# Half of the relu rounds of a recommendation tower move from ScalarE to VectorE, added to the round before

## The chip, the cores and the metric

The kernel runs on one core of a Trainium2 chip. Its time is the device time of one execution in microseconds; smaller is better. The time before is the median of three runs. One more execution was taken by the hardware profiler, and all rows below come from that one.

## The reference

2,048 samples, 16 fields each. Every field looks up a row of 256 floats in its own table, so a sample is a matrix `x` of 16 x 256. Three layers work on it:

```
xk = x
for i in range(3):
    z = einsum('bfe,bge->bfge', x, xk).reshape(B, 256, E)      # pairwise products of fields
    z = swapaxes(z, 1, 2)
    z = einsum('bcl,oc->bol', z, Ws[i]) + bs[i][None, :, None]  # here E = 256 is contracted with Ws[i]
    z = sum(relu(z), axis=-1)                                   # 16 numbers a sample
    outs.append(z)
    xk = broadcast(z[:, :, None], (B, 16, 256))
h = concatenate(outs + [dense_ctx]); two relu layers (512, 256) and one output
```

Layer 0 needs the products of fields with each other. Layers 1 and 2 (in the kernel k = 0 and k = 1) multiply `x` by a number per sample and field, so they need only the projection of `x` by the weights, an outer product with the previous `z`, the bias, relu, and a sum over all 16 x 16 pairs.

## The kernel before

The batch is worked in 128 steps of 16 samples; 8 steps make a group of 128 samples, 16 groups in all. All arithmetic is f32. The program is a hand-written software pipeline: each engine runs its own loop over "slots" 0 to 159, and in slot s it does its share for step s and, at fixed offsets, its share of the later stages of earlier groups. Engines meet only through semaphores; within an engine the order of the code is the order of execution. Because the offsets repeat every 8 slots, a slot's extra work depends on its number modulo 8.

For each step k:

- GpSimd gathers embedding rows by indirect DMA into `emb` (line 257), and does a small share of the products (lines 267 and 217).
- TensorE transposes them into the PSUM tile `turn_ps` (`turn`, line 483). It does this two slots ahead, as the first thing in its slot, and first waits until VectorE has done the products of the current slot, which read the same half of `turn_ps`.
- ScalarE copies `turn_ps` to `emb_t` (lines 398, 399) and makes the squares (line 406).
- VectorE makes the products (`products`, in `multiply`, line 217): 3,360 numbers per partition, one factor from `turn_ps` and one from `emb_t`.
- TensorE contracts them with the weights (`sum_pairs`, line 503, 32 matmuls), and ScalarE reduces the result with relu (`relu_pairs`, lines 416 and 419).

Layers 1 and 2 of a group are each cut into four rounds q = 0 to 3. In every slot from 14 on TensorE does one round (`outer_round`, lines 531 and 535): bias and outer product go into `outer_ps`, a PSUM tile of four banks of which only one copy exists, so the next round waits for `outer_relu`, the count of rounds already read. Round (k, g, q) is in slot 8g + 14 + q for k = 0 and 8g + 26 + q for k = 1, hence q = 1 and q = 3 always fall into odd slots. In the next slot ScalarE takes the result out with relu into `relu_k[:, k, q]` (`relu_round`, line 426; 4 x 256 numbers per partition). After the fourth round TensorE sums over rounds and over the four partitions that share a sample with a selector matrix `fold_sb` (`fold`, line 555) into `wide_ps`, and VectorE sums over fields (`reduce_fields`, line 369) into `z_cat`. GpSimd spreads `z_cat` into `z_wide` for the next layer (line 291).

`wide_ps` exists once. Its users follow each other in a fixed order, each waiting for the reader of the one before (`wait_wide`). By slot modulo 8:

| slot mod 8 | TensorE, beside turn, sums, one round | VectorE, behind `products` |
|---|---|---|
| 0 | `project` (line 546) | `reduce_fields` (k = 1) |
| 1 | `z_t` (line 517) ahead of the sums | `finish0` (lines 352, 355) |
| 2 | `fold` (k = 0) | `turn_proj` (line 363) |
| 3 | `z0` (line 514) ahead of the sums | |
| 4 | `hidden1` (line 563) | `reduce_fields` (k = 0) |
| 5 | `hidden2` (line 572) | |
| 6 | `fold` (k = 1) | |
| 7 | `y` (line 521) ahead of the sums | |

The order of an engine's slot is that of its loop. TensorE: `turn(slot + 2)`, side work, `sum_pairs(slot)`, `outer_round`, wide work. VectorE: `products(slot)`, then what the table's last column names. ScalarE reads the results of `hidden1` and `hidden2` one slot later (`relu_hidden`). ScalarE: `relu_round` of the slot before, `take_turned(slot + 2)`, `relu_hidden`, `squares(slot + 2)`, `relu_pairs(slot)`, side work. `prods` has three buffers. Products end with step 127; slots 128 to 159 only finish the last groups.

Of the kernel before, what the change touches and what calls it, by code (L numbers as in the profile page):

```python
# [11 lines left out]
ALU = mybir.AluOpType  # L12
# [7 lines left out]
F = 16  # L20
# [18 lines left out]
G4 = F // 4  # L39
# [20 lines left out]
ROUND_NO = {(k, g, q): n for n, (_, k, g, q) in enumerate(ROUND_ORDER)}  # L60
ROUND_AT = {s: (k, g, q) for s, k, g, q in ROUND_ORDER}
# [9 lines left out]
def group_at(slot, offset):  # L71

    g, rest = divmod(slot - offset, PER)
    return g if rest == 0 and 0 <= g < GROUPS else None


def at_least(eng, sem, value):

    if value > 0:
        eng.wait_ge(sem, value)  # L80


def build(nc, tables, ids_t, id_limits, ident, w_cols, biases, bias_rows, bias_parts, w_proj, own_field, row_mask,
          sample_mask, fold_sel, dense_t, w_top1, b_cols1, w_top2, b_cols2, w_top3, y_out):
    ctx = ExitStack()
    with ctx:
        def sb(name, shape, dt=FP32):
            return ctx.enter_context(nc.sbuf_tensor(name, shape, dt))

        def ps(name, shape):  # L90
            return ctx.enter_context(nc.psum_tensor(name, shape, FP32))

        def sem(name):
            return ctx.enter_context(nc.semaphore(name))
# [13 lines left out]
        relu_k = sb("relu_k", [P, 2, G4, J, F * F])  # L108
# [33 lines left out]
        outer_ps = ps("outer_ps", [P, J, 512])  # L142
# [30 lines left out]
        outer_done = sem("outer_done")  # L173
        outer_relu = sem("outer_relu")
        fold_done = [sem(f"fold_done{k}") for k in range(2)]
# [34 lines left out]
        def multiply(eng, k, b0, b1, own, done):  # L210

            x = emb_blocks(k)[:, b0:b1, :]
            step = [list(d) for d in x.ap]
            shifted = bass.AP(x.tensor, x.offset + 1, [step[0], step[1], [1, SHIFTS - 1], [1, F]])
            every = own.rearrange("p n (u f) -> p n u f", u=1).broadcast_to([P, b1 - b0, SHIFTS - 1, F])
            out = prod_blocks(k)[:, b0:b1, F:SHIFTS * F].rearrange("p n (s f) -> p n s f", f=F)
            eng.tensor_tensor(out, every, shifted, ALU.mult).then_inc(done, 1)  # L217
# [93 lines left out]
        def _(dve):  # L311
# [21 lines left out]
                                           in1=bias_part[:, 0, :], op0=ALU.mult, op1=ALU.add).then_inc(setup, 1)  # L333
            dve.wait_ge(setup, 9)
            nc.vector.scalar_tensor_tensor(out=rest_mid[:], in0=bias_lo[:], scalar=parts_sb[:, 2:3],
                                           in1=bias_part[:, 1, :], op0=ALU.mult, op1=ALU.add).then_inc(setup, 1)
# [4 lines left out]
            def products(k):  # L341

                if k < STEPS:
                    dve.wait_ge(emb_t_ready, 2 * (k + 1))
                    at_least(dve, sums_done, k - PRODS_RING + 1)
                    own = turn_ps[:, k % 2, :].rearrange("p (n f) -> p n f", f=F)[:, 0:VECTOR_BLOCKS, :]
                    multiply(nc.vector, k, 0, VECTOR_BLOCKS, own, prods_dve)

            def finish0(g):

                dve.wait_ge(relu0_ready, 3 * PER * (g + 1))
                nc.vector.tensor_reduce(own_sum[:], own0[:, g % 2, :, :], AX.X, ALU.add).then_inc(own_sum_ready, 1)
                dve.wait_ge(own_sum_ready, g + 1)
                at_least(dve, diag_ready, g - 1)
                nc.vector.scalar_tensor_tensor(out=z0_rows[:, g % 2, :], in0=pair_sum[:, g % 2, :], scalar=2.0,
                                               in1=own_sum[:], op0=ALU.mult, op1=ALU.add).then_inc(z0_ready, 1)

            def turn_proj(g):

                dve.wait_ge(proj_done, g + 1)  # L360
                if g >= PT_RING:
                    dve.wait_ge(outer_done, ROUND_NO[1, g - PT_RING, G4 - 1] + 1)
                nc.vector.transpose(proj_b[:, g % PT_RING, :].rearrange("p (f m) -> p f m", f=F),
                                    wide_ps[:].rearrange("p (s f) -> p f s", f=F)).then_inc(proj_ready, 1)

            def reduce_fields(k, g):

                dve.wait_ge(fold_done[k], g + 1)
                nc.vector.tensor_reduce(z_cat[:, g % CAT_RING, (k + 1) * F:(k + 2) * F],  # L369
                                        wide_ps[:, 0:F * F].rearrange("p (f o) -> p o f", o=F),  # L370
                                        AX.X, ALU.add).then_inc(z_ready[k], 1)

            for slot in range(LAST_SLOT + 1):
                products(slot)
                if (g := group_at(slot, Z0_FIN)) is not None:
                    finish0(g)
                if (g := group_at(slot, TURN_P)) is not None:
                    turn_proj(g)
                for k in range(2):
                    if (g := group_at(slot, REDUCE[k])) is not None:  # L380
                        reduce_fields(k, g)

        @block.scalar
        def _(act):
# [16 lines left out]
            def squares(k):  # L401

                if k < STEPS:
                    act.wait_ge(emb_t_ready, 2 * (k + 1))
                    at_least(act, sums_done, k - PRODS_RING + 1)
                    nc.scalar.square(prod_blocks(k)[:, :, 0:F], emb_blocks(k)[:, :, 0:F]).then_inc(squares_ready, 1)  # L406
# [15 lines left out]
            def relu_round(k, g, q):  # L422

                act.wait_ge(outer_done, ROUND_NO[k, g, q] + 1)
                at_least(act, fold_done[k], g)
                nc.scalar.activation(relu_k[:, k, q, :, :], outer_ps[:, :, 0:F * F], ACT.Relu).then_inc(outer_relu, 1)  # L426
# [32 lines left out]
            for slot in range(LAST_SLOT + 1):  # L459
                if slot == HIDDEN1:  # L460
                    act.wait_ge(top_in, N_TOP * 16)
                if slot - 1 in ROUND_AT:
                    relu_round(*ROUND_AT[slot - 1])
                take_turned(slot + 2)
                if slot - 1 in WIDE_AT:
                    relu_hidden(*WIDE_AT[slot - 1])
                squares(slot + 2)
                relu_pairs(slot)
                if slot in SIDE_AT:
                    take_side(*SIDE_AT[slot])  # L470

        @block.tensor
        def _(pe):
# [76 lines left out]
            def fold(k, g):  # L550

                pe.wait_ge(outer_relu, ROUND_NO[k, g, G4 - 1] + 1)
                for q in range(G4):
                    for j in range(J):
                        last = nc.tensor.matmul(wide_ps[j * R:(j + 1) * R, 0:F * F], fold_sb[:], relu_k[:, k, q, j, :],  # L555
                                                start=q == 0, stop=q == G4 - 1)
                last.then_inc(fold_done[k], 1)

            def hidden1(g):
# [96 lines left out]
```

## Time and profile before

| | us |
|---|---|
| median of 3 runs | 630.85 (630.07 to 631.62) |
| profiled execution, its own time | 628.34 |
| its span, first to last instruction | 626.6 |
| TensorE (PE) busy | 575.6 |
| VectorE (DVE) busy | 499.5 |
| ScalarE (ACT) busy | 455.3 |
| GpSimd (POOL) busy | 463.7 |

The span is what the trace covers; the execution's own time is 1.7 us longer. Busy times are of single engines and overlap each other. PEld, in some rows, is the load of weights into TensorE, beside the matmuls. "L217" is line 217 of the kernel before.

### The profile page before, as it was taken

What the parts mean: (1) busy time and instruction counts of PE and PEld (TensorE: products, weight loads), DVE (VectorE), ACT (ScalarE), POOL (GpSimd) and SP (SyncE); (2) the same over time, 40 slices, a digit from 0 to 9 for tenths busy, and PEclk for the clock granted to TensorE, in tenths of its full rate; (3) what the DMA queues carried; (4) which work ended last, traced back from release to release, by engine and by line L of the source; (5) the groups of instructions that cost most, each with busy time, mean ns of one, the idle gap of its engine ahead of it and who ended that gap; (6) DMA issues with size and microseconds to landing.
All of it is one profiled execution on the core that took longest, in us unless ns stands there. A gap on an engine that the chain in (4) does not pass through costs nothing.

```text
span 626.6 us, 19391 instructions
## 1 busy us (share of the span) xinstructions
PE 575.6 (92%) x7936; PEld 328.8 (52%) x7936; DVE 499.5 (80%) x220; ACT 455.3 (73%) x1298; POOL 463.7 (74%) x565
## 2 busy tenths in 40 slices
PE   2878798999999999999999999999999999997776
PEld 1444454555646555564656555565556555554354
DVE  5999999999898988889898988889888888941000
ACT  2666777787878787877887787777878788765542
POOL 6999999999988788888888888788878787621000
PEclk9999999999999999999999999999999999999988
DMA  3322222222222212222212122212212222100000
GB/s 97 112 73 73 69 70 68 70 70 65 69 64 61 61 58 63 61 61 62 65 56 65 57 61 60 69 55 68 60 55 67 61 61 57 47 3 1 1 1 2
DMA packets 14794, 35.97 MB, mean 57 GB/s; under 512 B 5922, under 2 KB 6306, under 8 KB 14690
## 3 DMA queue, kind: packets, MB, share of 16 engines
q0 software_dynamic: 12288, 33.57, 18.8%
q1 hardware_dynamic: 2418, 1.16, 0.7%
q8 instruction: 64, 1.05, 0.7%
q14 instruction: 24, 0.19, 0.1%
HBM read 34.70 MB, written 0.01 MB: 55 GB/s over the span
## 4 chain that ended last, share of the span: by engine, by line
PE 82%; POOL 8%; issue 4%; ACT 3%; DMA 1%; DVE 1%; SPq 0%; POOLq 0%
PE sum_ps L503 35%; PE turn_ps L483 10%; PE wide_ps L555 10%; PE outer_ps L535 8%; PE wide_ps L572 6%; PE wide_ps L546 4%; POOL emb L257 4%; PE outer_ps L531 4%; PE wide_ps L563 3%; POOL prods L267 2%; POOL prods L217 2%; ACT relu_k L426 1%; PE sum_ps L521 1%; PE sum_ps L517 1%; DVE prods L217 1%
## 5 line engine op out<-in xcount | busy, mean ns | idle before, releaser
L217 DVE TENSOR_TENSOR prods<-turn_ps,emb_t 128x3360 f32<-128x3360 f32 x128 | 466.1, 3655 | 55.1 <-ACT emb_t L399 52.2
L257 POOL DMA_INDIRECT emb<-tables,rows_sb x256 | 252.2, 985 | 45.4 <-issue 34.5
L503 PE MATMUL sum_ps<-prods,w_sb 128*32 128x272 f32 x4096 | 265.0, 397 | 18.6 <-POOL prods L217 11.1
L503 PEld LDWEIGHTS sum_ps<-prods,w_sb 128*32 128x32 f32 x4096 | 136.4, 110 | 103.6 <-issue 39.6
L426 ACT ACTIVATE relu_k<-outer_ps 128x1024 f32<-128x1024 f32 x128 | 132.4, 1035 | 11.2 <-PE outer_ps L535 11.1
L416 ACT ACTIVATE relu<-sum_ps,bias_sb 128x120 f32<-128x120 f32 x256 | 90.6, 361 | 58.4 <-PE sum_ps L503 57.2
L267 POOL TENSOR_TENSOR prods<-emb_t 128x256 f32<-128x256 f32 x128 | 95.3, 745 | 46.3 <-ACT emb_t L399 45.1
L398 ACT COPY emb_t<-turn_ps 128x512 f32<-128x512 f32 x128 | 75.3, 589 | 71.3 <-PE turn_ps L483 71.3
L483 PE MATMUL turn_ps<-ident_sb,emb 128*128 128x128 f32 x512 | 84.6, 289 | 12.7 <-DMA emb<-tables,rows_sb 10.0
L483 PEld LDWEIGHTS turn_ps<-ident_sb,emb 128*128 128x128 f32 x512 | 55.1, 142 | 60.5 <-issue 57.6
L406 ACT ACTIVATE prods<-emb_t 128x512 f32<-128x512 f32 x128 | 81.5, 637 | 3.3
L217 POOL TENSOR_TENSOR prods<-emb_t 128x224 f32<-128x224 f32 x128 | 77.5, 605 | 2.3
L535 PE MATMUL outer_ps<-proj_b,z_wide 32*128 32x256 f32 x1024 | 78.0, 378 | 0.0
L555 PE MATMUL wide_ps<-relu_k,fold_sb 128*32 128x256 f32 x1024 | 61.9, 382 | 1.5 <-ACT h L453 1.4
L291 POOL TENSOR_TENSOR z_wide<-z_cat,sample_sb 128x512 f32<-128x512 f32 x32 | 33.7, 1052 | 29.0 <-PE outer_ps L535 21.1
L369 DVE TENSOR_REDUCE z_cat<-wide_ps 128x16 f32<-128x256 f32 x32 | 13.4, 419 | 50.3 <-PE wide_ps L555 50.3
L416 ACT ACTIVATION_READ_ACCUMULATOR relu<-sum_ps,bias_sb 128x1 f32 x256 | 51.5, 201 | 0.0
L399 ACT COPY emb_t<-turn_ps 128x256 f32<-128x256 f32 x128 | 49.5, 386 | 0.0
L531 PE MATMUL outer_ps<-bias_wide,ones_sb 32*128 32x256 bf16 x512 | 37.0, 279 | 10.7 <-ACT relu_k L426 10.5
L531 PEld LDWEIGHTS outer_ps<-bias_wide,ones_sb 32*128 32x128 bf16 x512 | 12.9, 91 | 64.0 <-issue 52.7
L555 PEld LDWEIGHTS wide_ps<-relu_k,fold_sb 128*32 128x32 f32 x1024 | 30.3, 109 | 28.1 <-issue 9.3
L535 PEld LDWEIGHTS outer_ps<-proj_b,z_wide 32*128 32x128 f32 x1024 | 40.2, 186 | 0.0
(41 smaller groups left out, 284.3 us busy)
## 6 DMA issues: line engine op xcount, KB each, us to landing
emb<-tables,rows_sb POOLq DMA_INDIRECT x256
w_sb<-w_top SPq DMA_DIRECT2D x1, 512.0 KB, 4.3
ids_sb<-ids_t SPq DMA_DIRECT2D x1, 128.0 KB, 2.1
h<-dense_t SPq DMA_DIRECT2D x1, 128.0 KB, 2.9
w_sb<-w_top SPq DMA_DIRECT2D x1, 128.0 KB, 3.1
ident_sb<-ident SPq DMA_DIRECT2D x1, 64.0 KB, 2.1
w_sb<-w_cols SPq DMA_DIRECT2D x1, 64.0 KB, 1.9
wp_sb<-w_proj SPq DMA_DIRECT2D x1, 32.0 KB
```

Source lines behind the costliest of these rows:

```text
L217: eng.tensor_tensor(out, every, shifted, ALU.mult).then_inc(done, 1)
L257: nc.gpsimd.indirect_dma_start(out=emb[:, k % EMB_RING, t * E:(t + 1) * E], out_offset=None, in_=tables, in_offset=bass.IndirectOffsetOnAx ...
L267: nc.gpsimd.tensor_tensor(prod_blocks(k)[:, :, SHIFTS * F:], x[:, :, 0:SHIFTS], x[:, :, SHIFTS:F], ALU.mult).then_inc(prods_pool, 1)
L398: nc.scalar.copy(out[:, :, 0:F], src).then_inc(emb_t_ready, 1)
L406: nc.scalar.square(prod_blocks(k)[:, :, 0:F], emb_blocks(k)[:, :, 0:F]).then_inc(squares_ready, 1)
L416: nc.scalar.activation(relu0[:, t, :], sum_ps[:, t * PAIRS + F:(t + 1) * PAIRS], ACT.Relu, bias=bias_sb[:, 0:1], accum_out=pair_sum[:, g % ...
L426: nc.scalar.activation(relu_k[:, k, q, :, :], outer_ps[:, :, 0:F * F], ACT.Relu).then_inc(outer_relu, 1)
L483: last = nc.tensor.transpose(turn_ps[:, k % 2, i * P:(i + 1) * P], emb[:, k % EMB_RING, i * P:(i + 1) * P], ident_sb[:])
L503: last = nc.tensor.matmul(sum_ps[s * 2 * F:(s + 1) * 2 * F, 0:SUM_COLS], w_sb[:, c, odd, :], x[:, c, 2 * s + odd, :, :], start=c == 0 and ...
L531: nc.tensor.matmul(outer_ps[:, j, 0:F * F], ones_sb[j * R:(j + 1) * R, :], bias_wide[j * R:(j + 1) * R, k, :], start=True, stop=False)
L535: last = nc.tensor.matmul(outer_ps[:, j, 0:F * F], z_wide[j * R:(j + 1) * R, k, q, :], y[j * R:(j + 1) * R, k, :, :], start=False, stop=True)
L555: last = nc.tensor.matmul(wide_ps[j * R:(j + 1) * R, 0:F * F], fold_sb[:], relu_k[:, k, q, j, :], start=q == 0, stop=q == G4 - 1)
```

## The change

VectorE reads the rounds q = 1 and q = 3 out of `outer_ps`. One `scalar_tensor_tensor` takes the maximum with 0 and adds the relu of the round ahead, which ScalarE wrote to `relu_k[:, k, q - 1]`; the sum goes to `relu_k[:, k, q]`. It stands in VectorE's loop behind the products of the slot after the round. ScalarE keeps q = 0 and q = 2. `fold` reads only `relu_k[:, k, 1]` and `relu_k[:, k, 3]`, so 16 matmul instructions instead of 32 show for it in the trace.

```
+def on_vector(k, g, q):
+
+    return q % 2 == 1
...
+            def relu_add(k, g, q):
+
+                dve.wait_ge(outer_done, ROUND_NO[k, g, q] + 1)
+                dve.wait_ge(outer_relu, ROUND_NO[k, g, q])
+                at_least(dve, fold_done[k], g)
+                nc.vector.scalar_tensor_tensor(out=relu_k[:, k, q, :, :], in0=outer_ps[:, :, 0:F * F], scalar=0.0,
+                                               in1=relu_k[:, k, q - 1, :, :], op0=ALU.max, op1=ALU.add).then_inc(outer_relu, 1)
+
...
             for slot in range(LAST_SLOT + 1):
                 products(slot)
+                if slot - 1 in ROUND_AT and on_vector(*ROUND_AT[slot - 1]):
+                    relu_add(*ROUND_AT[slot - 1])
                 if (g := group_at(slot, Z0_FIN)) is not None:
...
-                if slot - 1 in ROUND_AT:
+                if slot - 1 in ROUND_AT and not on_vector(*ROUND_AT[slot - 1]):
                     relu_round(*ROUND_AT[slot - 1])
...
                 pe.wait_ge(outer_relu, ROUND_NO[k, g, G4 - 1] + 1)
-                for q in range(G4):
+                for q in range(1, G4, 2):
                     for j in range(J):
                         last = nc.tensor.matmul(wide_ps[j * R:(j + 1) * R, 0:F * F], fold_sb[:], relu_k[:, k, q, j, :],
-                                                start=q == 0, stop=q == G4 - 1)
+                                                start=q == 1, stop=q == G4 - 1)
```

## Rows read from the trace of the kernel before

**Rows 1.** The page's first part: busy us, share of the span, instructions.

```profile
PE 575.6 (92%) x7936; PEld 328.8 (52%) x7936; DVE 499.5 (80%) x220; ACT 455.3 (73%) x1298; POOL 463.7 (74%) x565
```

**Rows 2.** Waits, 175 to 547 us, TensorE's and VectorE's: us, times, longest.

```profile
PE sum_ps L503 <- ACT y_sb L439: 0.2, 1, 0.2
...
DVE prods L217 <- ACT emb_t L399: 44.2, 65, 1.4
```

**Rows 3.** Windows: length; busy PE, PEld, DVE, ACT, POOL; granted clock, DMA share, GB/s.

```profile
76.16:107.56 31.40, 27.79 (x402) 15.60 (x398) 30.53 (x14) 23.53 (x72) 28.58 (x35) 1.00 0.24 71
107.56:140.07 32.51, 32.27 (x482) 17.29 (x478) 31.14 (x14) 26.65 (x75) 29.70 (x37) 1.00 0.24 67
140.07:175.16 35.09, 34.88 (x496) 19.83 (x492) 31.02 (x14) 27.62 (x81) 31.82 (x39) 1.00 0.24 69
175.16:210.66 35.50, 35.28 (x504) 20.07 (x499) 31.09 (x14) 28.06 (x82) 28.93 (x35) 1.00 0.21 61
...
606.00:616.00 10.00, 9.14 (x76) 6.77 (x72) 0.34 (x1) 3.82 (x8) 0.00 (x0) 0.66 0.01 2
```

**Rows 4.** The chain, 300 to 345 us: start, duration, what.

```profile
302.01 0.59 PE turn_ps L483 x4
...
307.21 0.44 PE turn_ps L483 x4
...
310.27 1.86 PE wide_ps L555 x32
312.13 0.59 PE turn_ps L483 x4
...
315.74 0.59 PE turn_ps L483 x4
...
329.76 0.59 PE turn_ps L483 x4
...
333.10 0.58 PE turn_ps L483 x4
...
337.52 0.59 PE turn_ps L483 x4
```

**Rows 5.** Lines by form: shapes, count, busy us, mean ns, idle before.

```profile
L217 DVE TENSOR_TENSOR prods<-turn_ps,emb_t 128x3360 f32<-128x3360 f32 x128 | 466.1, 3655 | 55.1 <-ACT emb_t L399 52.2
...
L426 ACT ACTIVATE relu_k<-outer_ps 128x1024 f32<-128x1024 f32 x128 | 132.4, 1035 | 11.2 <-PE outer_ps L535 11.1
...
L369 DVE TENSOR_REDUCE z_cat<-wide_ps 128x16 f32<-128x256 f32 x32 | 13.4, 419 | 50.3 <-PE wide_ps L555 50.3
...
L332 DVE SCALAR_TENSOR_TENSOR bias_part<-bias_mid,parts_sb,bias_part 128x32 f32<-128x32 bf16 x1 | 0.3, 252 | 0.0
```

**Rows 6.** One line's instructions: duration in ns, least, median and greatest.

```profile
L355 DVE SCALAR_TENSOR_TENSOR z_rows<-pair_sum,own_sum x16: 174/176/555, 46.9 to 564.3; 128x16 f32<-128x16 f32 x16
```

**Rows 7.** Timeline of VectorE, early and at the last products: start, duration.

```profile
46.50 0.41 DVE L352 TENSOR_REDUCE own_sum<-own 128x16 f32<-128x256 f32 x1
...
47.03 3.65 DVE L217 TENSOR_TENSOR prods<-turn_ps,emb_t 128x3360 f32<-128x3360 f32 x1
50.60 0.71 DVE L363 STREAM_TRANSPOSE proj_b<-wide_ps 128x512 f32<-128x512 f32 x1
51.23 10.75 DVE L217 TENSOR_TENSOR prods<-turn_ps,emb_t 128x3360 f32<-128x3360 f32 x3
...
548.52 7.44 DVE L217 TENSOR_TENSOR prods<-turn_ps,emb_t 128x3360 f32<-128x3360 f32 x2 [0.33 <-ACT emb_t L399]
```

**Rows 8.** The chain, from the last sums to the end: start, duration, what.

```profile
560.78 2.01 PE sum_ps L503 x29
...
569.58 0.14 issue
...
570.45 1.86 PE wide_ps L555 x32
...
613.66 1.93 PE wide_ps L555 x32
```

## The prediction

> **What bounds the kernel now.** I read the page's busy row first [rows 1]: TensorE 92%, VectorE 80%, ScalarE 73%. Shares alone do not say who waits, so I took the table of waits over 175 to 547 us, where the kernel repeats itself [rows 2]. There TensorE waits 0.2 us in 372, VectorE 44.2 us, always for ScalarE's copy of the turned embeddings, which itself can only follow TensorE's turn. So TensorE is the bound in that stretch, and VectorE has slack. The windows, cut where VectorE starts `finish0` (once in 8 slots), say since when [rows 3]: 31.40 us, 32.51, 35.09, then 35.50 for every further 8 slots. In the first of these VectorE is busy 30.53 of 31.40, TensorE only 27.79; from the third on TensorE is full (34.88 of 35.09). The early part is thus already set by the product side (VectorE, GpSimd close behind), the long part by TensorE.
>
> The chain in the repeating part gives TensorE's slots [rows 4]. I call a slot by its number modulo 8; the distance between starts of its `turn` is its length. Slot 5 (its usual work, then `hidden2`) is 302.01 to 307.21, 5.20 us; slot 6 (`fold1`) 4.92; slot 7 (`y`, no wide work) 3.61; slot 3 329.76 to 333.10, 3.34; slot 4 4.42; all eight 302.01 to 337.52, 35.51.
>
> **Removed from TensorE.** A fold's 32 matmuls are 1.86 us of chain [rows 4] and become 16, 0.93. Two folds in 8 slots: TensorE's own period falls from 35.5 to 33.65. This is a true gain if TensorE stays the bound. Fewer reads of `relu_k` cost nothing elsewhere.
>
> **Removed from ScalarE.** 64 of 128 relus of 1.035 us [rows 5], 66 us. ScalarE was not the bound; its copies start when the turn ends, and I cost this at nothing: what hides it is TensorE's queue. In the new order VectorE's own queue hides it.
>
> **Added to VectorE.** 64 instructions over 128x1024 f32, one input in PSUM, one in SBUF. No such form is in the trace. From below: two VectorE operations that read PSUM give a slope of (3655 - 419) / (3360 - 256) = 1.0425 ns an element; 419 + 768 x 1.0425 = 1220 ns [rows 5]. From above: the same operation on 32 elements with a pointer scalar took 252 ns [rows 5], 219 beyond its elements, so 1.28 us. A duration under 1.035, ScalarE's own for this tile, has no row for it. I take 1.22, because this instruction has no pointer scalar. Back to back, VectorE starts the next instruction 0.08 us before the last one's end: products 47.03 to transpose 50.60 is 3.57 for 3.65, transpose to products 0.63 for 0.71 [rows 7]. So in the queue: products 3.57, new relu-and-sum 1.14, field reduction 0.33, transpose 0.63, `finish0` 0.53 (46.50 to 47.03 [rows 7]). Eight slots of VectorE, never waiting:
> 8 x 3.57 + 4 x 1.14 + 2 x 0.33 + 0.63 + 0.53 = 34.94 us.
> That is above TensorE's 33.65: VectorE becomes the bound, and the fold's saving is out of reach. By itself 34.94 would still be 0.56 less than 35.50.
>
> **The new wait.** The relu-and-sum of an odd slot's round stands on VectorE behind the products of the next slot and waits for TensorE's `outer_round`. Queued behind it are the next products, which TensorE's `turn` and `sum_pairs` need. So I followed one period, each engine in its order. TensorE in slot s starts its turn when the products of s are done, 0.13 to 0.14 us later (the 0.14 of "issue" ahead of TensorE in [rows 8]), or when its previous slot ends. I used the slot lengths above, with the fold shortened in slot 6 to 3.99; slots 0 to 2 together were 35.51 - 5.20 - 4.92 - 3.61 - 3.34 - 4.42 = 14.02 and are 13.09 now, against VectorE's 3 x 3.57 + 2 x 1.14 + 0.33 + 0.53 + 0.63 = 14.48.
> From slot 1 to slot 5 TensorE is thus ready before the products or just with them, and the round is done before VectorE gets to it. The closest is slot 3: its round ends 0.13 + 3.34 + 0.07 = 3.54 after its products' end, at 3.66 + 3.54 = 7.20 after their start; VectorE is free at 2 x 3.57 = 7.14. About 0.1 us of wait with a cold start of TensorE.
> Slot 5 is long (`hidden2`), and slot 6 has a fold. From the end of the products of slot 5, TensorE needs 0.13 + 5.20 + 3.99 + 3.61 + 0.07 = 13.00 us to the round of slot 7. VectorE gets there sooner: 3.57 + 1.14 + 3.57 + 3.57, less the 0.08 of overlap, = 11.77. It stalls some 1.2 us, once a period. What is late next: the reduction and the products of slot 1, then all of the queue up to the products of slot 5, for which TensorE waits. The loop closes:
> relu-and-sum 1.14, reduction 0.33, slot 1 3.57 + 0.53, slot 2 3.57 + 1.14 + 0.63, slot 3 3.57, slot 4 3.57 + 1.14 + 0.1 + 0.33, products of slot 5 3.66, then 13.00: 36.28 us.
> I take 36.3 against 35.5. The other waits of this edit are covered: `fold` needs the relu-and-sum 3.3 us after its slot's turn, and it and the transpose take 1.14 + 0.71; TensorE's `outer_round` needs it behind `sum_pairs` (2 us), and it takes 1.22. Both covers would fail only if it cost about 2 us. ScalarE's copies are ready over 1 us before VectorE asks.
>
> **The sum, against the profiled 628.34 (span 626.6).**
> Early, VectorE is full, so its work counts: the 8 slots to 76.16 get one of the new instructions, +1.1; the next 31.40 get two: busy 30.53 [rows 3] + 2.28 = 32.8, +1.4; the 32.51 get four, 34.9, +2.4. Together +4.9.
> From slot 34 to 127: 94 slots, 11.75 periods; the first 35.09 to 36.3, the other 10.75 by +0.8: 1.2 + 8.6 = +9.8.
> Behind the last products: VectorE ends them at 555.96 (548.52 + 7.44 [rows 7]), and TensorE ends the last sum at 562.79 (560.78 + 2.01 [rows 8]), 6.8 us behind, since it was the bound. With VectorE ahead by no more than one slot it is: slots 5 and 6 without their turns' 0.59 in slot 6, 0.13 + 5.20 + 3.40 + 0.42 + 2.0 = 11.15 after the products of slot 5; the last products end 8.28 after those. 2.9 behind, so -3.9.
> Tail: five folds on the chain, from 570.45 to 613.66 [rows 8], each -0.93, -4.65; of the relus there about five go to VectorE and pass on 1.22 instead of 1.035, +0.9. -3.7.
> Sum: 4.9 + 9.8 - 3.9 - 3.7 = +7.1. The profiled run lay 2.5 us under the median of 630.85; I add to the median: 638.0.
>
> **Rivals.**
> A. Queue order costs nothing: the stall behind slot 7 doesn't form, and the period is VectorE's bare 34.94. For it: TensorE has 34.94 - 33.65 = 1.3 us of slack in a period. Against: it is short in slots 5 to 7, where they come together. The two periods differ by 1.36 x 11.75 = 16.0: 622. This is the one on the other side; the break-even lies 7.1 / 11.75 = 0.60 under 36.3, at a period of 35.7: half of the stall would have to be absent.
> B. TensorE stays the bound, 33.65. It needs a relu-and-sum of (33.65 - 30.38) / 4 = 0.8 us in the queue, under every row: 2.65 x 11.75 = 31.1 less than mine, and 4.9 early, about 602.
> C. The new instruction runs at half the rate: 2.29 us, 1.07 more each. Three are in the loop: 39.5; 3.2 x 11.75 = 37.6, early 1 + 2 + 4 of them 7.5, five in the tail 5.3: 688. Against: the same operation with both inputs f32 in SBUF took 176 ns on 16 elements [rows 6]; at 1.04 ns an element the rest is 159, near the 152 of the reduction (419 - 267); at twice that, 143. That leans to full rate, by 17 ns only.
> The Trainium skill ("Vector Engine (DVE) Microarchitecture Reference", section "Points that are easy to get wrong") says that this instruction's layout halves its throughput with two SBUF sources that are not bf16. Here one source is in PSUM, so by its words the rule does not bite; if it holds for any second f32 source it gives C's time. The row of 176 ns, which has two such sources, does not agree with it clearly.
> D. Dearer hand-overs: no overlap at 1.28 us (+0.16 each, three in the loop) and 0.4 us of further restarts of TensorE: period 37.2, +0.9 x 11.75 = 10.6 and about 1.5 elsewhere: 650.
> That the change doesn't do what it says has no room: each operation stands in its engine's list.
>
> **Numbers.** Mine 0.60, own range 631 to 646; A 0.16; B 0.02; C 0.06; D 0.16. A and the low end of mine hold what ends faster or near zero. About 0.3% (2 us) is what a measurement here can tell from none. The relu-and-sum at 1.22 to 1.28 is +2.8 us on the sum, an overlap that fails +3.8. The tail may move too: TensorE's granted clock was 0.66 over 606 to 616 [rows 3], between its levels of 1.2 and 2.4 GHz; another pattern of waits there can be worth 2 or 3 us either way. Range 620 to 651, from A to D: outside lie C, B and edges. Faster 0.19 (A, B, a little of mine), same 0.09, slower 0.72.
>
> **What would show it.** VectorE busy about 577 us, over 90% of the span; the new line near 1.22 us; ScalarE near 389; the fold line with 512 matmuls and 31 us. In 175 to 547 us, TensorE should wait for VectorE's products several times a period, VectorE should be idle about 1.3 us a period, before the relu-and-sum, put down to `outer_round`; the 8-slot distance of `finish0` 36.3. The last sum should end about 3 us behind the last products. Wrong would make it: a period under 35.7, VectorE idle for ScalarE's copies as before, or another duration of the new line.

## The result and the profile after

The changed kernel took 654.79 us (median of 4, 653.66 to 656.76) against 630.8: 1.0383 of before, 95% interval 1.0354 to 1.0412, 24 us slower. The forecast was 638.0, up to 651. The direction was right and the loop that the forecast rests on is there, but the change cost over three times the 7.1 us that I had worked out. The same program, measured twice more, gave 1.0211 (1.0187 to 1.0235) and 1.0409 (1.0369 to 1.0449). About two thirds of what was missing is that difference, and the experiments below are mostly about it.

The busy row of the page and the forms that answer to [rows 1] and [rows 5]:

```profile
PE 553.2 (85%) x7424; PEld 308.2 (47%) x7424; DVE 566.2 (87%) x284; ACT 406.8 (62%) x1234; POOL 462.3 (71%) x565
```

```profile
L222 DVE TENSOR_TENSOR prods<-turn_ps,emb_t 128x3360 f32<-128x3360 f32 x128 | 461.9, 3644 | 3.0 <-ACT emb_t L414 3.0
L376 DVE SCALAR_TENSOR_TENSOR relu_k<-outer_ps,relu_k 128x1024 f32<-128x1024 f32 x64 | 78.3, 1224 | 57.2 <-PE outer_ps L550 57.1
...
L441 ACT ACTIVATE relu_k<-outer_ps 128x1024 f32<-128x1024 f32 x64 | 65.6, 1025 | 28.5 <-PE outer_ps L550 28.3
...
L570 PE MATMUL wide_ps<-relu_k,fold_sb 128*32 128x256 f32 x512 | 35.1, 393 | 1.5 <-ACT h L468 1.4
```

The new instruction took 1.224 us; the forecast had 1.22. TensorE's fold fell from 62 to 35 us busy (forecast 31), VectorE was busy 566 us (forecast 577), ScalarE 407 (forecast 389); nothing below rests on these three. VectorE's products no longer wait for ScalarE (3.0 us against 55.1 over the whole trace); its relu-and-sum waits 57 us for TensorE, 19.7 of them in the repeating part.

The waits over 175 to 547 us, as in [rows 2]:

```profile
PE turn_ps L498 <- DVE prods L222: 32.4, 49, 1.2
DVE relu_k L376 <- PE outer_ps L550: 19.7, 28, 1.5
...
ACT relu_k L441 <- PE outer_ps L550: 7.2, 29, 0.3
```

TensorE waited 0.2 us there before and now waits 32.4 for products, as forecast. VectorE, on whose queue these products stand, itself waits for TensorE's rounds. The timeline of VectorE over one period shows where:

```profile
297.70 3.65 DVE L222 TENSOR_TENSOR prods<-turn_ps,emb_t 128x3360 f32<-128x3360 f32 x1
301.29 1.22 DVE L376 SCALAR_TENSOR_TENSOR relu_k<-outer_ps,relu_k 128x1024 f32<-128x1024 f32 x1
302.43 0.71 DVE L368 STREAM_TRANSPOSE proj_b<-wide_ps 128x512 f32<-128x512 f32 x1
303.06 7.18 DVE L222 TENSOR_TENSOR prods<-turn_ps,emb_t 128x3360 f32<-128x3360 f32 x2
310.70 1.23 DVE L376 SCALAR_TENSOR_TENSOR relu_k<-outer_ps,relu_k 128x1024 f32<-128x1024 f32 x1 [0.45 <-PE outer_ps L550]
...
319.85 1.22 DVE L376 SCALAR_TENSOR_TENSOR relu_k<-outer_ps,relu_k 128x1024 f32<-128x1024 f32 x1 [0.47 <-PE outer_ps L550]
...
329.16 1.23 DVE L376 SCALAR_TENSOR_TENSOR relu_k<-outer_ps,relu_k 128x1024 f32<-128x1024 f32 x1 [0.96 <-PE outer_ps L550]
```

The four relu-and-sums stand in slots 2, 4, 6 and 0. The stall in slot 0 is the one of the forecast; those of 0.45 and 0.47 us in slots 4 and 6 are not in it, or only as 0.1. The distance between starts of `finish0` became 33.74, 32.87, 36.54, then 37.03 us (forecast 36.3) where it had been 29.66, 31.40, 32.51, 35.09 and 35.50.

Slot 4 stalls for the round that TensorE does in slot 3. The timeline of the same trace shows it, with a gather that GpSimd issues beside it:

```profile
309.32 0.98 POOL L262 DMA_INDIRECT emb<-tables,rows_sb  x1
...
309.61 0.61 PE L550 MATMUL outer_ps<-proj_b,z_wide 32*128 32x256 f32 x8
...
310.70 1.23 DVE L376 SCALAR_TENSOR_TENSOR relu_k<-outer_ps,relu_k 128x1024 f32<-128x1024 f32 x1 [0.45 <-PE outer_ps L550]
```

VectorE is free at 310.25, but the round is reported done only 1.07 us after the start of its matmuls. The next round, of slot 4, is read by ScalarE and shows the same at its largest, first in the timeline and then in the chain:

```profile
313.00 0.99 POOL L262 DMA_INDIRECT emb<-tables,rows_sb  x1 [0.16 <-issue]
313.05 0.60 PE L550 MATMUL outer_ps<-proj_b,z_wide 32*128 32x256 f32 x8
...
314.35 1.02 ACT L441 ACTIVATE relu_k<-outer_ps 128x1024 f32<-128x1024 f32 x1 [0.32 <-PE outer_ps L550]
```

```profile
313.21 1.11 PE outer_ps L550 x8
...
314.35 1.03 ACT relu_k L441
...
328.44 0.70 PE outer_ps L550 x8
```

A round's f32 matmuls are 0.44 us of chain in an undisturbed slot; here they are 1.11, because the reader was let go 1.30 us after their start. The trace also records the updates of the semaphore `outer_done`. In the kernel before all 102 rounds that could be paired with an update up to 530 us were reported done 0.66 us after the start of their f32 matmuls. In this trace 76 of 96 came later than 0.75 us, up to 1.30. I call them late rounds. Of the rounds that VectorE reads, those of slots 3, 5 and 7 were reported some 1.07, 1.20 and 0.85 us after their start.

### The profile page after: what moved, and what is told of

Read it like the earlier page. It is cut to its first block, busy times and chain, and to the rows that moved or that the text cites. A ratio compares the mean times of both kernels' runs of the same rounds, so it can differ in the third digit from the quotient of the medians.

```text
span 651.8 us, 18371 instructions
## 1 busy us (share of the span) xinstructions
PE 553.2 (85%) x7424; PEld 308.2 (47%) x7424; DVE 566.2 (87%) x284; ACT 406.8 (62%) x1234; POOL 462.3 (71%) x565
## 4 chain that ended last, share of the span: by engine, by line
PE 52%; DVE 32%; issue 8%; ACT 6%; POOL 1%; DMA 0%; SPq 0%; DVEq 0%
DVE prods L222 28%; PE sum_ps L518 24%; PE outer_ps L550 8%; PE turn_ps L498 6%; PE wide_ps L587 6%; ACT relu_k L441 4%; PE outer_ps L546 3%; PE wide_ps L570 3%; DVE relu_k L376 2%; ACT relu L431 1%; PE sum_ps L536 1%; DVE z_cat L382 1%; PE wide_ps L578 1%; DVE own_sum L357 1%; ACT h L462 1%
## 5 line engine op out<-in xcount | busy, mean ns | idle before, releaser
L518 PEld LDWEIGHTS sum_ps<-prods,w_sb 128*32 128x32 f32 x4096 | 130.4, 110 | 104.2 <-issue 35.2
L498 PE MATMUL turn_ps<-ident_sb,emb 128*128 128x128 f32 x512 | 83.0, 286 | 63.5 <-DVE prods L222 51.3
L376 DVE SCALAR_TENSOR_TENSOR relu_k<-outer_ps,relu_k 128x1024 f32<-128x1024 f32 x64 | 78.3, 1224 | 57.2 <-PE outer_ps L550 57.1
L441 ACT ACTIVATE relu_k<-outer_ps 128x1024 f32<-128x1024 f32 x64 | 65.6, 1025 | 28.5 <-PE outer_ps L550 28.3
L587 PE MATMUL wide_ps<-h,w_sb 128*128 128x128 f32 x256 | 36.8, 303 | 2.2 <-ACT h L462 2.1
L587 PEld LDWEIGHTS wide_ps<-h,w_sb 128*128 128x128 f32 x256 | 33.7, 212 | 8.1 <-ACT h L462 4.1
```

Of the source, the lines that this page charges most:

```text
L376: nc.vector.scalar_tensor_tensor(out=relu_k[:, k, q, :, :], in0=outer_ps[:, :, 0:F * F], scalar=0.0, in1=relu_k[:, k, q - 1, :, :], op0=AL ...
L498: last = nc.tensor.transpose(turn_ps[:, k % 2, i * P:(i + 1) * P], emb[:, k % EMB_RING, i * P:(i + 1) * P], ident_sb[:])
L518: last = nc.tensor.matmul(sum_ps[s * 2 * F:(s + 1) * 2 * F, 0:SUM_COLS], w_sb[:, c, odd, :], x[:, c, 2 * s + odd, :, :], start=c == 0 and ...
L587: last = nc.tensor.matmul(wide_ps[:, i * P:(i + 1) * P], w2_sb[:, a, i * P:(i + 1) * P], h1[:, a * P:(a + 1) * P], start=a == 0, stop=a == ...
```

## The experiments

Sixteen kernels in four batches (the recorded expectations say calls). All kernels of a batch ran on one chip, and each batch on another one, 4, 12, 13 and 1; the chip of the first measurement is not on record. Times are medians, with the ratio to the kernel before in the same batch.

**First batch: fold, wait and work by themselves.** `fold_only` is the kernel before with the fold of the changed one:

```
-                for q in range(G4):
+                for q in range(1, G4, 2):
...
-                                                start=q == 0, stop=q == G4 - 1)
+                                                start=q == 1, stop=q == G4 - 1)
```

> The kernel before, with the fold reading two rounds instead of four; ScalarE still takes out all four rounds, and half of each layer's sum is left out. Theory Q (in the changed kernel the fold's saving is real and is lost in VectorE's queue): TensorE is still the bound, the 8-slot period falls from 35.5 to 33.65 us, 11.75 periods give -21.9 and five folds in the tail -4.7: about 604 us. Rival F (the halved fold saves nothing on the path, another bound stands right behind TensorE): period 35.0 or more, 620 to 628 us.

605.32 us, 0.9612 (0.9585 to 0.9638), period 33.87. The fold's saving is real: 24 us, as long as nobody else has to pay for it. The period is a little above the 33.65 worked out: a halved fold takes 1.00 us of chain in the traces, not 0.93 (1.86 before).

`wait_only` is the kernel before with the waits alone:

```
                 products(slot)
+                if slot - 1 in ROUND_AT and ROUND_AT[slot - 1][2] % 2 == 1:
+                    dve.wait_ge(outer_done, ROUND_NO[ROUND_AT[slot - 1]] + 1)
```

> The kernel before, with only the wait added: VectorE waits for the round of every second slot at the place of the new instruction, and does nothing there. Before, VectorE starts the products about two slots ahead of TensorE's sums; the wait forbids that. Theory Q (occupancy and wait together close a loop): the wait alone costs the lead once, 2 to 4 us, period 35.5: 631 to 635 us. Rival W (waiting in VectorE's queue for TensorE is what costs): period near 37, 648 us or more. Second question: in the changed kernel a round is reported done 0.66 to 1.3 us after its start, before always 0.66; if a VectorE that stands waiting for that semaphore makes the report late, ScalarE's relus wait here as well.

634.71 us, 1.0088 (1.0062 to 1.0114). The time is in the range; the first 8 slots with a wait grew from 29.66 to 32.66 us, and in the repeating part the period was 35.84, where 35.5 was expected. The timeline shows the first wait:

```profile
58.27 14.34 DVE L217 TENSOR_TENSOR prods<-turn_ps,emb_t 128x3360 f32<-128x3360 f32 x4
75.49 3.66 DVE L217 TENSOR_TENSOR prods<-turn_ps,emb_t 128x3360 f32<-128x3360 f32 x1 [2.88 <-PE outer_ps L537]
```

VectorE had run ahead of TensorE; the wait takes this lead away at once. The changed kernel has the same 2.82 us before its first relu-and-sum, at 75.32 us. 48 of 101 rounds were late here, which did not settle the second question by itself: `fold_only` had 55 late rounds of 105 with no wait in VectorE's queue at all. A waiting VectorE is not their cause.

`work_only` is the kernel before with an instruction of VectorE that waits for nobody:

```
                 products(slot)
+                if slot - 1 in ROUND_AT and ROUND_AT[slot - 1][2] % 2 == 1:
+                    nc.vector.tensor_reduce(spare_out[:], spare_in[:], AX.X, ALU.add)
```

> The kernel before, with only occupancy added: at the place of the new instruction VectorE does a reduction over 128x1024 in SBUF, some 1.22 us, that waits for no other engine and whose result is not used. Theory Q: VectorE's own period is 34.94, below 35.5; early +4.9, a little more in the period where its copies come late: 635 to 641 us. Rival O (VectorE's occupancy alone explains the loss): 650 us or more.

632.60 us, 1.0046 (1.0022 to 1.0070), period 35.6: a little under what was expected. Occupancy alone costs 3 us, the wait alone 5; both together cost 13 to 27 in the three measurements, with a cheaper fold at that. The two do not simply add: the work makes the loop longer that the wait has closed.

`round_early` changes TensorE's order in the changed kernel:

```
                 turn(slot + 2)
+                ahead = slot in ROUND_AT and on_vector(*ROUND_AT[slot])
+                if ahead:
+                    outer_round(*ROUND_AT[slot])
                 if slot in SIDE_AT:
                     side(slot, *SIDE_AT[slot])
                 sum_pairs(slot)
-                if slot in ROUND_AT:
+                if slot in ROUND_AT and not ahead:
                     outer_round(*ROUND_AT[slot])
```

> The changed kernel, with TensorE doing the round of odd slots, the ones VectorE takes out, ahead of that slot's sums instead of behind. All work stays. Theory Q: VectorE finds every round done, its three stalls of 0.45, 0.5 and 0.95 us a period go, the period falls from 37.04 to VectorE's bare 34.94 to 35.3, 11.75 x 1.9 = 22 us: 629 to 634 us. Rival O (occupancy, or contention on the path of the new instruction): within 3 us of 654.8.

639.55 us, 1.0169 (1.0141 to 1.0197): 15 us better than the 654.8 of the changed kernel, with all work kept, so occupancy alone is not the cause; but it is above the range, and the period is 36.5, not 35.3. By spans, 3.7 of the 15 us lie before slot 34, 8.0 in slots 34 to 127 and 3.3 behind. The edit changes two things at once: the wait of VectorE, and whether its rounds are late. Of the rounds moved behind the turn 2 of 48 were late, of those still behind the sums 43 of 49. The chain shows what took the place of the wait:

```profile
358.79 2.05 PE sum_ps L518 x29
...
361.66 0.18 ACT own L434
361.84 0.13 ACT y_sb L454
361.97 0.14 issue
362.11 2.04 PE sum_ps L518 x32
```

Without the round behind them, the sums of slot 7 end at 360.84 and the next ones, at 362.11, wait for ScalarE to read them: the round had covered that read.

**Second batch.** `no_gather` is the changed kernel with gathers for the first `EMB_RING` pairs alone:

```
-                if k < STEPS:
-                    if t == 0:
-                        at_least(pool, turned, k - EMB_RING + 1)
+                if k < EMB_RING:
...
-                    pe.wait_ge(gathered[k % EMB_RING], PAIR * 16 * (k // EMB_RING + 1))
+                    pe.wait_ge(gathered[k % EMB_RING], PAIR * 16)
```

> The changed kernel, with the gathers of embeddings left out behind the first six steps, so that later steps use old rows. Theory G (a round is reported done late, up to 1.3 instead of 0.66 us after its start, when a gather's descriptors are being made on GpSimd at that time; in the changed kernel's trace the late ones have such an instruction running beside them, and behind the last gather all are at 0.66): VectorE's stalls in slots 4 and 6 go and the one in slot 0 stays, the period is the 36.3 us of the prediction, 0.75 x 11.75 = 9 less: 644 to 647 us. Rival S (the lateness belongs to the order of work on TensorE and VectorE): period 37.0, within 2 us of 654.8.

638.47 us, 1.0171 (1.0145 to 1.0196), period 36.37. All stalls of VectorE but that of slot 0 were gone. Against the 654.79 of the changed kernel that is 16.3 us, of which the period gives (37.03 - 36.37) x 11.75 = 7.8. The time is 5.5 us below theory G's range. It looked like a clear yes to it all the same, until the next kernel took the argument away; and against the changed kernel without late rounds, measured later (1.0211), the missing gathers are worth some 0.4% at most.

`full_fold` is the changed kernel with the whole fold:

```
-                for q in range(1, G4, 2):
+                for q in range(G4):
...
-                                                start=q == 1, stop=q == G4 - 1)
+                                                start=q == 0, stop=q == G4 - 1)
```

> The changed kernel with the old fold over all four rounds (the first and third round are then counted twice). Theory Q (the period is a loop that runs through VectorE's queue up to the products of slot 5 and then through TensorE's slots 5, 6 and 7, with one fold in it): +0.93 a period, 10.9, and up to 4.7 in the tail: 668 to 671 us. Rival O (VectorE is the bound by itself, TensorE's slots do not count): the tail alone, 657 to 660 us.

654.86 us, 1.0435 (1.0387 to 1.0482), about as slow as the changed kernel had been in the first measurement and below both ranges. It lay nearest to the rival's, and I nearly took it for that. Its trace says otherwise: no late round among 97, with the gathers in place, VectorE's only stall in slot 0 (2.16 us), and period 37.24, the 36.38 of the loop without late rounds (third batch, below) and 0.86 for the other half of the fold. Two effects of the same size had been compared with each other across batches. So late rounds were in every kernel of the first batch and, with `no_gather` not to be judged, in no kernel of the second.

`fourth_only` is the changed kernel with `return q == 3` in `on_vector` and `for q in (0, 1, 3)` in `fold`; `fourth_early` has the order of `round_early` as well.

> VectorE takes out only the fourth round of each layer, added to the third; the fold reads three. Theory Q: VectorE's own period is 30.38 + 2 x 1.14 = 32.7, TensorE's 35.5 - 0.93 = 34.57, so TensorE stays the bound and the stall behind slot 7 does not exist: 630.8 - 0.93 x 11.75 + about 2.5 early - 2 in the tail: 619 to 623 us. Rival W (any wait for TensorE in VectorE's queue costs more than a quarter of a fold gives): above 631 us.

631.69 us, 1.0043 (1.0019 to 1.0067), period 35.60, a clear miss of 10 us. The chain:

```profile
327.27 0.04 DVE relu_k L376
...
328.42 0.71 DVE proj_b L368
...
332.59 3.65 DVE prods L222
336.24 0.14 issue
336.38 0.63 PE turn_ps L498 x4
```

and TensorE's timeline the turn of slot 3, which is not on the chain:

```profile
332.81 0.63 PE L498 MATMUL turn_ps<-ident_sb,emb 128*128 128x128 f32 x4 [0.81 <-DVE prods L222]
```

VectorE is not the bound over the period (32.7), but between TensorE's round of slot 1 (done at 327.25) and its turn of slot 3 there stand only one short slot of TensorE and relu, transpose and products of VectorE. The turn of slot 4, at 336.38, waits 0.18 us more. TensorE waited 9.9 us for products over 180 to 530 us.

> The same with the fourth round done ahead of that slot's sums on TensorE. Theory Q: the wait of VectorE is gone but was not in the path: within 2 us of the run before, 618 to 623 us. Rival (the late report of rounds is in the path): 4 us or more below it.

622.82 us, 0.9931 (0.9907 to 0.9956), period 35.31: 9 us below, more than either side had said for it without late rounds (there was none). No round was late in either kernel, so late rounds play no part here: the wait of VectorE (22.9 us over 180 to 530 in `fourth_only`, 6.8 here) had been in the path after all. By spans, 2.8 us of the gain lie before slot 34, 4.0 in slots 34 to 127 and 2.1 behind. What is left is again ScalarE's read behind sums that nothing covers: `PE sum_ps <- ACT h` 7.4 us in 10 waits.

**Third batch: is it the chip or the program?**

> The kernel before once more, for its trace. In the runs so far the late report of rounds (0.8 to 1.3 instead of 0.66 us after their start, each with a gather being issued beside it) is in all four kernels of the first call and in the changed kernel, and in none of those of the second call, where gathers stood just as near. Theory M (it belongs to the chip or the moment, not to the kernel): all kernels of this call have it or none has. Rival K (it belongs to the program): the kernel before has none, the changed kernel has it, full_fold_again has none. Time as before in either case, because ScalarE comes to the rounds later than that.

> The changed kernel once more. If the rounds are reported late: period 37.0, 3.8% over before. If none is late: the 36.3 of the loop worked out in the prediction, about 8 us less, 1.025 to 1.030 of before.

> The changed kernel with the old fold once more. In the first run no round was late and the period was 37.24, which is the loop's 36.3 plus one fold half of 0.93. If none is late again: 37.24, and 0.9 us a period above after_again, some 11 to 15 us in all. If rounds are late: 37.9.

The kernel before took 628.14 us and had no late round. The changed kernel took 641.61 us, 1.0211 (1.0187 to 1.0235), with none of 99 late, and period 36.38; the ratio is a little below what had been expected for that case. `full_fold_again` took 657.68 us, 1.0453 (1.0424 to 1.0482), with none late and period 37.24, 16 us above `after_again` where 11 to 15 had been expected. Rival K, a property of the program, is out: one program had 76 late rounds and then none. This is the timeline of VectorE in the changed kernel without them:

```profile
305.96 1.22 DVE L376 SCALAR_TENSOR_TENSOR relu_k<-outer_ps,relu_k 128x1024 f32<-128x1024 f32 x1
...
314.56 1.22 DVE L376 SCALAR_TENSOR_TENSOR relu_k<-outer_ps,relu_k 128x1024 f32<-128x1024 f32 x1
...
324.21 1.23 DVE L376 SCALAR_TENSOR_TENSOR relu_k<-outer_ps,relu_k 128x1024 f32<-128x1024 f32 x1 [1.30 <-PE outer_ps L550]
```

and the chain, which runs from the products of slot 5 through TensorE's slots 5, 6 and 7 to the round of slot 7:

```profile
307.51 3.58 DVE prods L222
311.09 0.14 issue
311.23 0.63 PE turn_ps L498 x4
...
314.48 1.98 PE wide_ps L587 x16
316.46 0.44 PE turn_ps L498 x4
...
319.53 1.00 PE wide_ps L570 x16
320.53 0.59 PE turn_ps L498 x4
...
323.70 0.44 PE outer_ps L550 x8
...
332.64 0.49 PE outer_ps L550 x8
...
333.35 0.05 DVE relu_k L376
```

Up to here it is the loop of the prediction. From the round of slot 7 that loop goes on over VectorE: the relu-and-sum at 324.21, then its queue without a gap, 1.14 + 0.33 + 3.57 + 0.53 + 3.57, to the relu-and-sum of slot 2 at 333.35. The chain as drawn goes over TensorE's slots 0 and 1 to the same instruction. The round before it ends at 333.13, so that way is only some 0.2 us shorter: there are two loops of nearly the same length, of which the prediction had worked out one.

One stall, 1.30 us (worked out: 1.23), slots 4 and 6 without one, 36.38 us (36.28). And slot 4, whose gather stands where it stood in the late one:

```profile
308.66 0.98 POOL L262 DMA_INDIRECT emb<-tables,rows_sb  x1 [0.16 <-issue]
308.71 0.60 PE L550 MATMUL outer_ps<-proj_b,z_wide 32*128 32x256 f32 x8
309.59 1.03 ACT L441 ACTIVATE relu_k<-outer_ps 128x1024 f32<-128x1024 f32 x1
```

Here the reader starts 0.88 us after the matmuls' start, there 1.30.

`pick_slots` asks whether the room between the round and TensorE's next need is the rule for where to put such work:

```
-    return q % 2 == 1
+    return q == (1, 3)[k]          # fold: (1, 2, 3) for k = 0, (0, 1, 3) for k = 1
```

> VectorE takes out one round of a layer, but in the layer k = 0 the second and in k = 1 the fourth, so that its instruction stands in slots 0 and 6, where TensorE has project and comes from hidden2. In fourth_only it stood in slot 2: there relu-and-sum, transpose, products and the hand-over are 1.14 + 0.63 + 3.66 + 0.13 = 5.56 us against TensorE's 4.77 for that slot, and TensorE lost the difference. Here 1.14 + 0.33 + 3.66 + 0.13 = 5.26 stand against 5.22, and slot 6 follows hidden2: theory Q: period TensorE's own 34.6 to 34.8, 617 to 622 us, 6 to 10 us under fourth_only. Rival (it is the amount of work on VectorE, not its place): the same as fourth_only.

624.38 us, 0.9950 (0.9933 to 0.9968), period 35.20: better than `fourth_only` by 0.4 us a period, but above the range. TensorE still waits for the products of slot 2, 5.2 us in 10 waits over 180 to 530. I had compared the work of one slot and not of two: the right sum, made before the next run, gives VectorE 9.43 us against TensorE's 8.79.

**Fourth batch.**

> The changed kernel a third time. With late rounds: period 37.0, 1.036 to 1.041 of before. With none: 36.38 and 1.019 to 1.024, as in the second measurement.

> The kernel before with half a fold, again, for its trace. Its first trace had 55 of 105 rounds late. Theory M: late here only if the changed kernel's rounds are late in this call. Without lateness the period is TensorE's 33.65, against 33.87 in the first.

The changed kernel took 656.02 us, 1.0409 (1.0369 to 1.0449), with 73 of 96 rounds late; `fold_only_again` took 607.42 us with 53 of 106 late and period 33.85. So in this batch all have them again, in kernels with and without the new instruction: theory M stands. Since every batch had its own chip, chip and moment can't be told apart.

> The changed kernel with the odd rounds ahead of the sums, again. In the first measurement ScalarE took the even rounds late and so the odd ones started late: period 36.5. Theory Q without lateness: VectorE's waits shrink further, period 35.0 to 35.6, 9 to 15 us under the changed kernel of this call. With lateness: 36.5 again, 15 us under it as before.

636.89 us, 1.0121 (1.0086 to 1.0155), period 36.45, 45 of 100 rounds late: as in the first batch, 19 us under the changed kernel of this one. What it would be without late rounds was not measured.

`pick_wide` is `pick_slots` with `return q == (2, 3)[k]` and the fold over (0, 2, 3) for k = 0:

> One round of a layer on VectorE, the third in k = 0 and the fourth in k = 1, which stand in slots 0 and 5, where TensorE has project and hidden2 right behind the round. From the end of the round of slot 0 to its turn in slot 2 TensorE has 1.86 + 3.57 = 5.43 us; VectorE needs 0.07 + 1.14 + 0.53 + 3.66 + 0.13 = 5.53. In pick_slots it was 0.07 + 1.14 + 0.33 + 3.57 + 0.53 + 3.66 + 0.13 = 9.43 against 5.22 + 3.57 = 8.79, the 0.5 us that TensorE lost there. Theory Q: period 34.6 to 34.8, 0.4 to 0.6 under the 35.20 of pick_slots: 0.982 to 0.989 of before. Rival (amount of work, not place): 35.2, 0.995.

623.06 us, 0.9875 (0.9837 to 0.9914), period 34.72, although half of its rounds (51 of 102) were late. TensorE waited for products once over 180 to 530 us, 0.9 us. The chain through slots 0 and 1 is TensorE alone:

```profile
353.22 1.85 PE wide_ps L561 x16
355.07 0.59 PE turn_ps L498 x4
355.66 0.35 PE sum_ps L532 x2
```

Of the versions that do all of the reference's work this has the lowest ratio, 1.2% under the kernel before; its interval just touches that of `fourth_early`, and it was measured in one batch only. It gives VectorE half as much as the change did and puts it behind the two rounds that TensorE follows with its longest work.

## Why the prediction was right, and wrong

**What bounds each kernel.** Right. `fold_only` shows that TensorE was the bound before (33.87 for the 33.65 worked out) and the waits after that VectorE's queue took over.

**The price of the instruction.** Right: 1.224 us for 1.22. Rival C is out. The Trainium skill's remark on halved throughput with two SBUF sources that are not bf16 ("Vector Engine (DVE) Microarchitecture Reference", "Points that are easy to get wrong") speaks of two SBUF sources only, and with one source in PSUM this trace shows no halving; no run here tried two SBUF sources at this size.

**The loop.** Right: 36.38 us for 36.28 and one stall of 1.30 for 1.23, where no round was late; one more fold half gave 37.24, +0.86; and taking VectorE's wait away made `fourth_early` faster than `fourth_only` with no late round in either. The fold's term was a little too good, 1.00 us for 0.93, and the 0.1 of stall in slot 4 did not form without late rounds; the two nearly cancel. Rival A is out, since the stall forms. Rival B needed a cheaper instruction. Rival D came nearest to the first measurement in number (period 37.2, 650 us), but not by its reasons: the instruction took 1.22 us and the next one started 1.14 behind it (310.70 to 311.84), and TensorE's turn started 0.13 us behind the products as before.

**The step that failed.** "its round ends 0.13 + 3.34 + 0.07 = 3.54 after its products' end": the 0.07 between TensorE's last matmul and the release of its reader. In the first measurement it was some 0.5 us for the round of slot 3, 0.6 for slot 5 and 0.25 for slot 7. The relu-and-sums that wait for the rounds of slots 3 and 5, for which the prediction had 0.1 us of stall and none, then stalled 0.45 and 0.47. The kernel before had no late round in its traces, and its ScalarE came to most rounds later than their report anyway, so nothing in it could show this. The price: 0.65 us a period, 37.03 against the 36.38 without late rounds. The sum by `finish0` starts and span, in us, each trace against a trace of the kernel before (the third batch's against its own):

| | forecast | first measurement | third batch |
|---|---|---|---|
| 24 slots up to slot 33 | +4.9 | +9.6 | +7.5 |
| slots 34 to 127 | +9.8 | +19.3 | +11.0 |
| behind the last products, and tail | -7.6 | -3.4 | -5.2 |
| all | +7.1 | +25.3 | +13.3 |

(In the first measurement the first `finish0` came 0.2 us sooner than before, which is in the last line alone.) The two measurements differ by 2.1 us in the first line, 8.3 in the second and 1.8 in the third; 7.6 of the second are the 0.65 a period. One period of the first measurement was 38.67 us long instead of 37.03, with a granted clock of 0.96 in that window, so not all of the difference need be late rounds. And without any late round the change still cost 13.3 us for 7.1: 2.6 more early, 1.2 more in slots 34 to 127, 2.4 less gained behind.

**The early part was mis-sized too.** "the 8 slots to 76.16 get one of the new instructions, +1.1": it was +4.1 and +3.7. The instruction's own 1.14 is there, and beside it 2.8 us of VectorE's lead, which `wait_only` shows by itself. The part asked what the instruction costs and not what its wait forbids.

**The tail.** Forecast -3.7 behind the last sum. Measured +0.3 in the first trace (the last sum ends at 587.65, 64.2 us before the end; before it was 562.73 and 63.8), and -1.4 in the third batch (62.3 for 63.7). The windows over the tail, after and before:

```profile
585.00:652.00 67.00, 47.13 (x490) 29.47 (x482) 15.54 (x19) 20.17 (x49) 3.57 (x4) 0.85 0.00 1
```

```profile
560.00:626.60 66.60, 47.75 (x574) 30.10 (x562) 3.86 (x9) 29.42 (x58) 3.57 (x4) 0.92 0.01 1
```

The granted clock is a mean over its two levels, 0.85 for 0.92: more of the tail ran at 1.2 GHz. In the third batch, where the tail lost less, it was 0.89 for 0.92. This fits a clock that took back part of what the folds gave; that it is the cause, and the whole of it, was not tested. That VectorE would be only 3 us ahead of TensorE at the end (2.9 worked out) was right: 584.66 and 587.65.

The range was missed by 4 us. The third batch, without late rounds, gave 641.6, inside the range; but its kernel before ran in 628.6, so that the change cost 13.0 us there, nearly twice the forecast. That the time itself lies 0.6% from the point is in part luck.

## What to carry to other kernels

Work moved to an engine with free time is paid by its place in that engine's queue, not by its share of the span: follow one period from each new wait to the next thing that the awaited engine needs from the same queue, and sum both sides over all slots between. A wait also takes away whatever lead the engine had, at once and for good. Before comparing two variants whose difference is about a per cent, look at the traces of both for the same disturbance, and repeat the reference kernel in the same batch, on the same chip.

## What the runs showed of the hardware

A matmul group's completion can be reported late. In nine traces, those of the first measurement and of two of the four batches, this holds up to 530 us: of 490 rounds that TensorE did behind the sums and that had an indirect DMA being issued on GpSimd from their start to at least 0.3 us behind it, 488 were late, up to 1.36 us after the start of their f32 matmuls, and half of them 0.35 to 0.4 us after that GpSimd instruction's end (for the round of slot 4 shown above 0.94 + 0.33). Of the 316 other rounds behind the sums 12 were late.

In the nine other traces, of the other two batches and both of the kernel before, the same overlaps were there (in all but `no_gather`, which has none) and every round came at 0.66. Kernels of one batch agreed in this without exception, eight with and seven without. The new instruction and its wait are not needed for it: `fold_only` has 55 late rounds. Whether the kernel before has them on the chips of the first and fourth batch was not traced.

Two things narrow it. First, it is not a matter of the rounds alone. In the nine traces with late rounds, 24 to 49 of 113 to 125 `sum_pairs` were reported over 0.25 us behind the modelled end of their last matmul as well; in the nine others none was. So what goes with late rounds may in part be late sums, whose reader is ScalarE. Second, the overlap is not enough. In `round_early` and `round_early_again` 25 rounds stood behind the turn instead of the sums and had a gather running 0.3 us or more past their start, and only 3 of them were late, where 86 of 86 behind the sums were. What the sums in front have to do with it was not tested.

The next matmuls start as without it (`hidden1` 0.53 us after the start of the round of slot 4 in the one trace, 0.54 in the other): it is the report, or the last writes, that is late. Which of the two it is, and what makes a batch have it, stays open. Between the two traces of the changed kernel, with 76 late rounds and with none, lie 12.3 us of span (651.8 and 639.5), not all of it by late rounds, as said above. Kernels whose readers come late anyway can have little of it in their time: the kernel before ran in 629.6 and 629.4 us in the batches with late rounds, and in 628.5 and 628.6 in those without.
